# Scaling of the scores of pairs 3 and 7 on VectorE for both heads, with the engines' lists and the PSUM bank table rearranged

## The reference

```python
h = layernorm(x) * (1 + ca) + sa
x = x + ga * attention(h)      # rmsnorm; 16 heads of 64; causal softmax; sigmoid gate per head; Wout
h = layernorm(x) * (1 + cb) + sb
x = x + gb * ffn(h)            # silu(h Wg + bg) * (h Wu + bu) Wd + bd, plus 512 experts:
                               # product keys, 4 heads, top 8 of 64 and 64, top 8 of the sums,
                               # silu(h . down[idx]) * softmax(scores), summed over up[idx]
```

## Time and profile before

| | |
|---|---|
| Time, median of 3 runs | 1404.91 us (1401.65 to 1404.97) |
| Profiled execution | 1400.69 us, of which the span from first to last instruction 1398.8 us |
| TensorE busy | 1369.1 us, 98% of the span; granted clock 1.00 |
| ScalarE busy | 1264.6 us, 90% |
| VectorE busy | 1214.9 us, 87% |
| GpSimd busy | 1080.4 us, 77% |
| Chain that ended last | TensorE 93%, VectorE 3%, ScalarE 2%, issue 1%, GpSimd 1% |
| DMA | 27.74 MB, mean 20 GB/s |

### The profile page before, as it was taken

How to read it: one execution, slowest core, us unless ns; L and a number is a source line. 1 busy time by engine, 2 the same in 40 slices (tenths; PEclk the granted TensorE clock), 3 DMA queues, 4 the chain that set the end, 5 groups by cost and what they waited for, 6 DMA issues and landing times.

```text
span 1398.8 us, 39734 instructions
## 1 busy us (share of the span) xinstructions
PE 1369.1 (98%) x11491; PEld 1157.3 (83%) x11491; DVE 1214.9 (87%) x5314; ACT 1264.6 (90%) x4212; POOL 1080.4 (77%) x1252
## 2 busy tenths in 40 slices
PE   6899999999999999999999999999999999999998
PEld 4778888888888888888888888888888888888877
DVE  6688898988898988898988898988898988898877
ACT  6889999999999999999999999999999999999975
POOL 2158888888888888888888888888888888888770
DMA  4000000000000000000000000000000000000000
GB/s 137 16 19 19 17 10 20 21 21 17 15 9 21 21 21 17 15 9 21 21 21 17 15 9 21 21 21 17 15 9 21 21 21 17 15 9 24 11 15 11
DMA packets 51042, 27.74 MB, mean 20 GB/s; under 512 B 10337, under 2 KB 50209, under 8 KB 51009
## 3 DMA queue, kind: packets, MB, share of 16 engines
q1 hardware_dynamic: 50768, 26.91, 7.3%
q10 hardware_dynamic: 240, 0.43, 0.1%
HBM read 23.02 MB, written 4.31 MB: 20 GB/s over the span
## 4 chain that ended last, share of the span: by engine, by line
PE 93%; DVE 3%; ACT 2%; issue 1%; POOL 1%; DMA 0%; SPq 0%; DVEq 0%; POOLq 0%
PE pW L1580 12%; PE pS L1648 12%; PE pW L1582 10%; PE pW L1581 10%; PE pW L1661 9%; PE pW L1689 8%; PE pS L1638 8%; PE pS L1634 7%; PE pW L1731 4%; PE pW L1734 4%; PE pW L1665 4%; PE pW L1722 2%; PE pW L1594 2%; ACT pS L693 1%; DVE pS L1126 0%
## 5 line engine op out<-in xcount | busy, mean ns | idle before, releaser
L693 ACT ACTIVATE pS<-pS,nmx 128x128 f32<-128x128 f32 (+1 forms) x1024 | 390.0, 437 | 31.3 <-DVE nmx L1126 30.7
L525 POOL TENSOR_TENSOR fexp<-fexp,fsum 128x512 f32<-128x512 f32 x240 | 316.5, 1347 | 90.6 <-DVE fexp L1277 90.6
L1126 DVE CUSTOM_DVE_ANT_0 pS<-pS,mask 128x128 f32<-128x128 f32 (+1 forms) x1024 | 332.3, 387 | 51.4 <-PE pS L1638 49.4
L516 POOL TENSOR_TENSOR fsum<-ex 128x512 f32<-128x512 f32 x248 | 251.8, 1047 | 1.3 <-ACT ex L741 1.3
L685 ACT COPY pT<-pS 128x768 f32<-128x768 f32 x256 | 206.1, 817 | 24.1 <-PE pS L1648 23.8
L1648 PE MATMUL pS<-ident,p_sb 128*128 128x128 f32 x1536 | 206.7, 274 | 6.8 <-DVE p_sb L1151 6.6
L1151 DVE TENSOR_TENSOR p_sb<-pS,coef 128x256 f32<-128x256 f32 (+2 forms) x512 | 208.9, 449 | 4.5
L693 ACT ACTIVATION_READ_ACCUMULATOR pS<-pS,nmx 128x1 f32 x1024 | 198.4, 194 | 0.0
L1648 PEld LDWEIGHTS pS<-ident,p_sb 128*128 128x128 f32 x1536 | 175.2, 141 | 27.6 <-DVE p_sb L1151 8.5
L1661 PE MATMUL pW<-pT,v 128*64 128x256 f32 x1024 | 162.3, 395 | 0.1
L1277 DVE TENSOR_SCALAR fexp<-fsum,top,rz 128x512 f32<-128x512 f32 x240 | 156.3, 702 | 0.0
(11 more groups left out here) (211 smaller groups left out, 3674.0 us busy)
## 6 DMA issues: line engine op xcount, KB each, us to landing
x_in<-in_L_attn_tokens SPq DMA_DIRECT2D x32, 128.0 KB, 2.1
x_res<-in_L_attn_tokens SPq DMA_DIRECT2D x32, 128.0 KB, 2.8
modB<-mods_dram SPq DMA_DIRECT2D x32, 128.0 KB, 2.9
modA<-mods_dram SPq DMA_DIRECT2D x31, 128.0 KB, 3.1
out<-yo SPq DMA_DIRECT2D x31, 128.0 KB, 1.9
modC<-mods_dram SPq DMA_DIRECT2D x32, 64.0 KB, 3.1
fsum<-in_L_attn_Wkv SPq DMA_DIRECT2D x1, 512.0 KB, 6.4
w_out<-in_L_attn_Wout SPq DMA_DIRECT2D x1, 512.0 KB, 7.3
```

Of the source, the lines that this page charges most:

```text
L516: ins = nc.gpsimd.tensor_tensor(fsum[:, k, h], ex[:, k, h, 0:NX].unsqueeze(2).broadcast_to([P, NX, NK]), ex[:, k, RH + h, :].unsqueeze(1). ...
L525: ins = nc.gpsimd.tensor_tensor(fexp[:, k, h, :], fexp[:, k, h, :], fsum[:, k, h].rearrange("p i j -> p (i j)"), ALU.mult)
L693: ins = nc.scalar.activation(ps, ps, ACT.Exp, bias=nmx[:, p % 2, h, k:k + 1], scale=-1.0, accum_out=den(p)[:, h, k:k + 1])
L1126: ins = nc.vector.tensor_tensor_reduce(out=ps, in0=ps, in1=mask[:, (1 - k) * P:2 * P], scale=-1.0, scalar=LARGEST, op0=ALU.add, op1=ALU.mi ...
```

## The change

`SHARED` is cut from pairs 1, 3, 5 and 7 to pairs 1 and 5. For pairs 3 and 7 `normalise` on VectorE then scales both heads (two instructions on 128 x 256 and 128 x 512 elements in place of 128 x 128 and 128 x 256), and ScalarE's `scale_head(3)` and `scale_head(7)` are gone from the steady list and from the list of iteration 0. The steady lists of GpSimd, ScalarE, VectorE and TensorE are put in another order, and so is `order`, the table that gives the banks. The lists of iterations -1, 0 and 32 are otherwise the same, as are the loop's bounds and SyncE's list. No other instruction is added or removed.

```diff
--- before.py
+++ after.py
@@ -41,7 +41,7 @@
 NW = 4
 BANK = 512
 NMOD = 7
-SHARED = (1, 3, 5, 7)
+SHARED = (1, 5)
 SA, CA, GA, GD, GB, COL = range(NMOD - 1)
 
 
@@ -233,11 +233,11 @@
         y_gated = ev("y_gated", 1)
 
 
-        order = [("GU", 1, -2), ("D", 0, -2), ("V", 0, 0), ("PV", 6, -1), ("PV", 7, -1), ("V", 3, 0), ("QK", 2, 0),
-                 ("V", 4, 0), ("QK", 3, 0), ("QK", 4, 0), ("D", 1, -2), ("QK", 5, 0), ("V", 5, 0), ("GU", 2, -2),
-                 ("V", 1, 0), ("op", 0, -1), ("QK", 6, 0), ("GU", 3, -2), ("PV", 0, 0), ("PV", 1, 0), ("PV", 2, 0),
-                 ("hT", 0, -1), ("PV", 3, 0), ("QK", 7, 0), ("ET", 0, -2), ("V", 2, 0), ("sim", 0, -1),
-                 ("sim", 1, -1), ("PV", 4, 0), ("PV", 5, 0), ("xT", 0, 1), ("y", 0, -2), ("ET", 1, -2),
+        order = [("V", 3, 0), ("V", 0, 0), ("PV", 6, -1), ("PV", 7, -1), ("QK", 2, 0), ("QK", 3, 0), ("D", 0, -2),
+                 ("V", 1, 0), ("V", 4, 0), ("GU", 1, -2), ("op", 0, -1), ("V", 5, 0), ("QK", 4, 0), ("GU", 2, -2),
+                 ("GU", 3, -2), ("QK", 5, 0), ("D", 1, -2), ("PV", 0, 0), ("PV", 1, 0), ("hT", 0, -1), ("PV", 2, 0),
+                 ("PV", 3, 0), ("QK", 6, 0), ("V", 2, 0), ("QK", 7, 0), ("sim", 0, -1), ("ET", 0, -2),
+                 ("sim", 1, -1), ("PV", 4, 0), ("PV", 5, 0), ("y", 0, -2), ("ET", 1, -2), ("xT", 0, 1),
                  ("GU", 0, -1), ("QK", 0, 1), ("QK", 1, 1)]
         assert len(order) % NW == 0, len(order)
         bank_of, off_of, place, count = {}, {}, {}, {}
@@ -616,17 +616,17 @@
 
                 products(0)
                 candidates()
+                add_bias()
                 products(1)
-                rstd1()
-                add_bias()
                 weigh(0)
                 add_heads(0)
+                rstd2()
+                rstd1()
                 fold(0)
-                rstd2()
-                rms1()
                 weigh(1)
                 add_heads(1)
                 fold(1)
+                rms1()
                 shift_top()
             run(pool, body)
 
@@ -832,7 +832,6 @@
                     weighted(1)
                     exp_scores(3)
                     queries(4)
-                    scale_head(3)
                     copy_transposes(2, 0)
                     values(4)
                     copy_transposes(3, 0)
@@ -855,7 +854,6 @@
                     exp_scores(7)
                     weighted(5)
                     queries(0)
-                    scale_head(7)
                     copy_transposes(6, 0)
                     queries(1)
                     down_weights()
@@ -904,61 +902,59 @@
                     return
 
 
-                gate_up(1)
-                down_tanh(0)
                 copy_transposes(7, -1)
+                values(3)
                 values(0)
                 exp_scores(0)
                 weighted(6)
-                values(3)
                 weighted(7)
+                exp_scores(1)
                 queries(2)
-                values(4)
-                exp_scores(1)
+                scale_head(1)
                 queries(3)
-                queries(4)
-                down_tanh(1)
-                scale_head(1)
+                down_tanh(0)
                 copy_transposes(0, 0)
                 copy_transposes(1, 0)
-                queries(5)
+                gate_up(1)
+                values(1)
+                exp_scores(2)
+                exp_scores(3)
+                values(4)
+                queries(4)
                 values(5)
                 gate_up(2)
-                exp_scores(2)
-                exp_scores(3)
+                gate_up(3)
+                queries(5)
                 total(0)
-                values(1)
-                gate_up(3)
-                scale_head(3)
-                queries(6)
+                down_tanh(1)
+                rows2()
                 copy_transposes(2, 0)
+                copy_transposes(3, 0)
+                modulate_h()
                 weighted(0)
-                rows2()
-                copy_transposes(3, 0)
                 weighted(1)
+                high_part(h2T_high, h2T, "hT")
                 exp_scores(4)
-                modulate_h()
                 weighted(2)
-                high_part(h2T_high, h2T, "hT")
                 weighted(3)
                 exp_scores(5)
+                queries(6)
                 queries(7)
+                values(2)
                 scale_head(5)
                 copy_transposes(4, 0)
                 experts(0)
-                values(2)
                 copy_transposes(5, 0)
-                rms_scale()
-                weighted(4)
                 expert_exp(0)
                 total(1)
+                exp_scores(6)
+                exp_scores(7)
+                experts(1)
+                weighted(4)
+                rms_scale()
                 weighted(5)
-                exp_scores(6)
+                high_part(xT_high, xT, "xT")
                 expert_exp(1)
-                high_part(xT_high, xT, "xT")
-                experts(1)
-                exp_scores(7)
-                scale_head(7)
                 gate_up(0)
                 copy_transposes(6, 0)
                 queries(0)
@@ -1462,72 +1458,72 @@
 
 
                 top_candidates()
+                row_max(0)
+                row_max(1)
+                invert(0)
+                sum_top()
+                invert_top()
                 ln1(stats1)
-                bias_product(1)
-                ln1(aggregate1)
-                gate_product(1)
-                sum_top()
-                gated_down(0)
-                row_max(0)
-                invert_top()
-                row_max(1)
-                ln1(center1)
+                coefficients(0)
+                normalise(0)
+                invert(1)
+                coefficients(1)
+                normalise(1)
                 choose(0, 0)
                 choose(0, 1)
-                invert(0)
-                ln1(scale1)
-                coefficients(0)
-                invert(1)
-                normalise(0)
-                coefficients(1)
-                normalise(1)
-                ln1(shift1)
-                gated_down(1)
-                choose(1, 0)
+                gated_down(0)
                 row_max(2)
+                bias_product(1)
                 row_max(3)
                 invert(2)
                 coefficients(2)
+                gate_product(1)
                 normalise(2)
-                bias_product(2)
+                ln1(aggregate1)
                 invert(3)
-                gate_product(2)
+                coefficients(3)
                 gate_attention()
                 add_residual()
-                coefficients(3)
                 stats2()
                 aggregate2()
-                ln1(square1)
                 normalise(3)
+                bias_product(2)
                 bias_product(3)
+                gate_product(2)
                 gate_product(3)
+                choose(1, 0)
                 choose(1, 1)
+                ln1(center1)
+                gated_down(1)
                 row_max(4)
+                low_part(h2T_high, h2T, "hT")
                 row_max(5)
                 invert(4)
-                low_part(h2T_high, h2T, "hT")
                 coefficients(4)
                 normalise(4)
                 invert(5)
                 coefficients(5)
                 normalise(5)
                 row_largest(0)
+                shift(0)
                 row_largest(1)
-                shift(0)
                 row_max(6)
+                ln1(scale1)
+                ln1(shift1)
                 shift(1)
+                row_max(7)
                 invert(6)
+                ln1(square1)
                 coefficients(6)
-                row_max(7)
                 normalise(6)
+                gate_output()
                 invert(7)
+                finish()
+                low_part(xT_high, xT, "xT")
                 coefficients(7)
-                low_part(xT_high, xT, "xT")
-                gate_output()
-                finish()
+                normalise(7)
                 bias_product(0)
                 gate_product(0)
-                normalise(7)
                 if first:
                     split_rest()
 
@@ -1913,56 +1909,56 @@
                     return
 
 
-                gate_up(1)
-                project_down(0)
+                project_v(3)
                 transpose_scores(7, -1)
                 project_v(0)
                 scores(0)
                 scores(1)
                 weigh_values(6)
                 weigh_values(7)
-                project_v(3)
                 project_qk(2)
+                project_qk(3)
+                project_down(0)
+                project_v(1)
                 project_v(4)
-                project_qk(3)
-                project_qk(4)
-                project_down(1)
-                project_qk(5)
-                project_v(5)
-                gate_up(2)
```

(21 more changed lines are left out.)

## The result

The changed kernel takes **1409.59 us** (median; 1406.81 to 1410.62) against 1404.93 in the same comparison, a ratio of 1.0034 with an interval of 1.0024 to 1.0044. The forecast was 1396.8. It is slower by just over what the measurement can tell, where I had said faster.

What follows compares the result with a forecast made beforehand. TensorE's instruction stream, with pauses and waits, was taken to bound the kernel. Terms of -0.55, -0.50 and +0.77 gave -0.28 us a period, times 29 -8.1 us: 1396.8 us against the median 1404.91, range 1382 to 1414.

Steps and rivals of the forecast that it cites:

- The bound: Steady part: TensorE's instruction stream plus pauses at changes of form plus waits sets the period, 41.985 us.
- Part 1: Scaling of pairs 3 and 7: ScalarE -1.48, VectorE +0.80 us an iteration, hidden by TensorE, nothing on the path.
- Part 2: TensorE's order at pairs 4 and 5: three changes of form fewer and a shorter pause, together -0.55 us a period.
- S5's wait: Scores of pair 5 wait for ScalarE's copy of pair 3's transposes: +0.15 us a period.
- pause ahead of S2: Change of form ahead of pair 2's scores, now behind a gate job: 0.20 for 0.25 us, saving 0.05.
- Part 3: Old waits at gate_up(3), pair 0's queries/keys and values(2) removed: -0.50 us a period, bounds -0.5 and 0.
- Part 4: New waits of TensorE behind the steps that are moved: +0.77 us a period, bounds 0.2 and 1.6.
- The end of the iteration: TensorE waits for the experts' copy (+0.43), xT (+0.03) and gate_up(0)'s bank (+0.11): sum +0.57 us a period.
- VectorE's gated_down and ScalarE's queries(2) ahead of values(4): New wait ahead of values(4) in TensorE's list: 0.05 us a period.
- B: The end of the iteration takes all back: waits 1.0, period 41.9 to 42.1, 1403 to 1408 us; chance 0.20.
- C: Slower: VectorE has no slack from row_max(2) to row_max(4), choose(1, 0) may overlap GpSimd; 1426 us, lesser 1412; chance 0.22.
- A: The order pays in full: new waits only 0.2 to 0.4, -0.75 us a period, 1383 us; chance 0.20.

Runs made afterwards that it cites:

- run 1: Kernel before with pairs 3 and 7 scaled wholly on VectorE, every list otherwise in the old order: 1408.17 us, ratio 1.0023.
- run 9: Kernel before with only pair 7 scaled wholly on VectorE: 1404.95 us, ratio 1.0004.
- run 2: Changed kernel with all four pairs still shared, so the new order alone: 1411.62 us, ratio 1.0053.
- run 5: Changed kernel with the old sequence of forms at pairs 4 and 5, VectorE's low part of hT behind row_max(5) and invert(4): 1469.86 us, ratio 1.0454.
- run 10: Kernel before with VectorE's bias_product(2) and gate_product(2) earlier and the low part of xT ahead of normalise(6): 1397.65 us, ratio 0.9942.
- run 3: Changed kernel with queries(2) ahead of exp_scores(1) in ScalarE's list: 1419.42 us, ratio 1.0105.
- run 7: Kernel before, unchanged, profiled once more: 1406.78 us in one run.
- run 6: Changed kernel with the transposes of pair 3 ahead of the values products of pairs 0 and 1 on TensorE: 1407.28 us, ratio 1.002.
- run 8: Kernel before with VectorE's bias_product(2) and gate_product(2) ahead of coefficients(2) and normalise(2): 1396.9 us, ratio 0.9948.
- run 11: Kernel before with the gate product earlier, low part of xT ahead of normalise(6), and pair 7 scaled wholly on VectorE: 1390.91 us, ratio 0.9906.

## Why the prediction was wrong, point by point

**The bound** was right: the time is TensorE's stream plus pauses plus waits, and the differences above were found in its weight loads. ScalarE's 1.16 us a period less bought no shorter period.

**Part 1, the scaling at nothing**, was wrong for the old order (+0.10, runs 1 and 9) and about right in the new one, where it even gives 0.05 (run 2). I had compared totals of a period (37.5 and 38.0 of 42), and what counts is the cover at one pair.

**Part 2, the forms**, held: T3 to QK6 takes 4.16, and my 3.98 plus 0.15 of wait make 4.13. The three changes are worth 0.50 and S5's wait 0.18 (run 5). The pause ahead of S2 fell by 0.06 for my 0.05 (gate_up(1)'s interval is 0.20 longer than gate_up(2)'s; in before values(1)'s was 0.26 longer than values(4)'s).

**Part 3, the old waits.** gate_up(3)'s 0.27 and some 0.1 at values(2) went. QK0's did not: T6's interval is 0.81 for 0.79 before. I had put it down as gone by the walk alone; run 10 shows that it needed an edit of its own.

**Part 4, new waits.** The end of the iteration was about half of what I took: y waits 0.34 (interval of its gated half) for my 0.43; xT and gate_up(0) wait 0 for my 0.14, and with xT's shorter interval 0.30 is left of the 0.57. (A slip of mine there: 5.82 and 0.27 for weighted(4) are 6.09, not 5.96. It would have made xT later still, and it was not late.) The step that failed is the last one, "VectorE's gated_down and ScalarE's queries(2) ahead of values(4)", which I put at 0.05. It is **0.49** by the interval that it ends, and 0.42 over the two jobs. Its chain begins with row_max(0), 2.33 us after T7's first load, and runs without a gap over ScalarE's exp_scores(0), two copies, exp_scores(1) and queries(2). I had added up the end of the iteration instruction by instruction and this chain not, though it is of the same kind. Run 3 shows that exchanging two of its steps doesn't remove the wait: it moves to the next job that needs ScalarE.

**The sum by rows.** Passage -0.33, gate_up(3) -0.26, values(2) -0.1, pause ahead of S2 -0.06, y and xT +0.30, values(4) +0.42, and one wait that I had not seen, PV0's, +0.09: +0.06; measured +0.08 against the first profile and +0.04 against run 7. PV0's load shows 0.26 idle where a plain change of form has 0.17:

```profile
624.51 0.23 PEld L1657 LDWEIGHTS pW<-pT,v 128*64 128x64 f32 x4 [0.26 <-issue]
```

Its bank is that of gate_up(2), and VectorE's gate_product(2), which frees it, now stands behind normalise(3); the trace names no engine, so this cause is argued. Against my -0.28 the result is 0.36 worse. values(4) alone makes 0.37 of that: had it been 0.05, the period would have been 41.69, against my 41.70. But this is luck in part, since my other errors nearly cancel: the end of the iteration costs 0.27 less than I took, while the old waits gave back 0.14 less and PV0's wait of 0.09 was missing.

**Outside the steady part** I had taken nothing. Span less the 29 periods is 1408.1 - 1219.77 = 188.3 us, for 181.2 in the first profile and 186.3 in run 7. After has three stretches at 1.2 GHz ahead of iteration 2, as run 7 has; at run 7's price 5.0 of the 7.1 us are thus the clock, in both kernels, and 2.0 are the change's. 0.75 of these lie in iteration 1 (output projection to output projection 42.52 us for 41.77 in run 7), where TensorE waits for xT, whose layer norm the new order has late, and falls to 1.2 GHz behind it (timeline of after, then its table by stretches):

```profile
94.96 0.69 PE L1590 MATMUL pW<-ident,xr 128*128 128x128 f32 x2 [4.21 <-ACT xr L774]
```

```profile
94.95:98.30 3.35, 3.34 (x16) 3.35 (x17) 1.98 (x5) 2.21 (x7) 3.35 (x4) 0.50 0.42 118
```

Where the other 1.3 lie depends on the mark. From the output projection of iteration 31 to the end it is 76.9 us in after and in runs 2, 3 and 6, for 75.0 to 75.2 in both profiles of before and in runs 1, 8, 9 and 11 (76.4 in run 10). But the new order itself puts the output projection 1.9 us further ahead of y. From y's first load over the experts in the same iteration to the end it is 53.4 for 54.1 to 54.2 us (55.5 in run 10), so by that mark the end is shorter and the loss lies in the opening. With 1.7 us for each stretch at 1.2 GHz ahead of iteration 2 (5.0 for three, run 7), the kernels of runs 2, 3 and 6 are 1.1 to 1.5 us above the first profile of before outside the steady part, and those of runs 1, 8, 9 and 11 between 0 and 0.5 below; run 10 is 1.5 above. So the loss goes with the new order; what in it makes it is open, and a run that isolates it wasn't made.

**The rivals.** B had the period (41.9 to 42.1) but by another cause: its place was the end of the iteration, with 1.0 of waits, and that takes 0.34. Its time, 1403 to 1408, was still too low by what lies outside the steady part. C is refuted: `choose` is at 544 ns and the transposes of pairs 4 and 5 have the intervals of before within 0.05. A is refuted by y's wait and values(4)'s. What I had called a sign of success, `choose` off GpSimd's long instructions, came true; that it is worth nothing was not measured by itself.

## What to carry to other kernels

When a list is dealt anew around a saturated engine, walk every chain whose consumer moves, by instructions, not only the one that looks tight: here one wait costed at 0.05 by feel was 0.42 to 0.49 and outweighed the gain. Totals per period say nothing about cover; try each edit on the old order alone, and where a removed wait returns a job later, look which engine's stretch feeds the new waiter and make that lighter (runs 10 and 11). Small edits in place beat the new order: 0.9906 for 1.0034.

## What the runs showed of the hardware

- The idle stretch at a change of form is 0.17 to 0.33 us in every kernel where nothing else is waited for. The Trainium skill (TensorEngine Tiling, section Tiling Modes) says that a change of mode drains TensorE; the runs agree, with 0.50 us a period for three changes less (4.49 us for 3.98 without S5's wait, run 5).
- The same waits of TensorE in the opening, 1.6 and 2.8 us, were followed by stretches at 1.2 GHz in one execution of the kernel before and by none in another. The difference is 5.0 us, more than the change itself, so one profile is no base for a forecast within 0.3%.
- Four of VectorE's `choose` instructions take 1.91 us where GpSimd is idle, and two took 2.32 beside its long multiplications. In the new order none stands beside these, the mean falls from 702 to 544 ns, and VectorE has 1.3 us more a period. The period is no shorter for it, though no run isolates this.
